# An S6 scan kernel on one Trainium2 core: the residual is added in PSUM by TensorE and copied out by ScalarE, where VectorE added it before

## What is computed

```
x = x + s6(layernorm(x))
x = x + ffn(layernorm(x))      # a routed feed-forward block on 127 rows of each batch

# s6: delta, B and C are projections of its input u
h = exp(delta * A) * h + delta * B * u     # 16 states for each of 512 channels, along 1024 steps
y = sum over states of h * C  +  u * D
```

## Time and profile before

| | |
|---|---|
| median of 3 runs | 4733.67 us (4727.59 to 4733.85) |
| the profiled execution's own time | 4730.44 us |
| its span in the profile | 4728.3 us |
| DVE busy in the span | 3868.9 us, 82% |
| POOL busy | 3543.6 us, 75% |
| PE busy | 2806.7 us, 59% |
| ACT busy | 2752.0 us, 58% |
| mean granted TensorE clock | 0.663 |

### The profile page before, as it was taken

The page is one execution under the profiler, slowest core; times in us unless marked ns, Lnnn a source line. Parts: engine busy times, 40 slices in busy tenths (PEclk is TensorE's granted clock), DMA queues, the critical chain, the costliest instruction groups (busy, mean ns, idle before and its releaser), DMA issues. The chain is left out here.

```text
span 4728.3 us, 57323 instructions
## 1 busy us (share of the span) xinstructions
PE 2806.7 (59%) x15590; PEld 1068.8 (23%) x15590; DVE 3868.9 (82%) x3306; ACT 2752.0 (58%) x4103; POOL 3543.6 (75%) x1796
## 2 busy tenths in 40 slices
PE   3555464546464645555454546464642399999997
PEld 1111111111121111111111111111110255555553
DVE  3999999999999999999999999999997644444442
ACT  5676766766767667676766766767754222222221
POOL 4999999999999999999999999999995100000000
PEclk7556565656565656556565656565655599999998
DMA  4454545364544545454545364545533200000000
GB/s 101 96 130 116 142 104 154 85 160 100 147 114 129 131 112 133 111 130 116 141 105 155 82 160 100 146 112 133 135 93 114 82 14 18 18 18 18 18 18 7
DMA packets 198209, 472.73 MB, mean 100 GB/s; under 512 B 60688, under 2 KB 61200, under 8 KB 197088
## 3 DMA queue, kind: packets, MB, share of 16 engines
q1 hardware_dynamic: 177136, 452.11, 37.8%
q0 software_dynamic: 20736, 16.88, 1.3%
HBM read 126.83 MB, written 73.43 MB: 42 GB/s over the span
## 5 line engine op out<-in xcount | busy, mean ns | idle before, releaser
L879 POOL TENSOR_TENSOR ch<-hid,cmat 128x1024 f32<-128x1024 f32 x1024 | 2387.2, 2354 | 101.0 <-DVE hid L733 84.1
L733 DVE TENSOR_TENSOR_SCAN hid<-decay,inp 128x1024 f32<-128x1024 f32 x1024 | 2289.2, 2274 | 96.3 <-ACT decay L600 94.2
L600 ACT ACTIVATE decay<-delr,a_neg 128x1024 f32<-128x1024 f32 x1024 | 1136.7, 1112 | 811.8 <-DVE hid L733 801.0
L399 PE MATMUL ps_y<-ch,nsum 128*32 128x256 f32 x8192 | 1000.3, 588 | 854.9 <-POOL ch L879 850.9
L722 DVE TENSOR_TENSOR inp<-dx,bmat 128x1024 f32<-128x1024 f32 x832 | 959.3, 1211 | 63.2 <-ACT dx L608 63.2
L399 PEld LDWEIGHTS ps_y<-ch,nsum 128*32 128x32 f32 x8192 | 249.0, 143 | 1591.5 <-POOL ch L879 1364.2
L408 PE MATMUL ps_y<-ident,ysb 128*128 128x128 f32 x512 | 168.9, 431 | 683.3 <-ACT ysb L615 666.7
L844 POOL TENSOR_TENSOR inp<-dxr,bmat 128x1024 f32<-128x1024 f32 x192 | 452.4, 2356 | 0.0
L1133 POOL DMA_INDIRECT out_rows<-row,idx_out x16 | 41.1, 2570 | 458.9 <-issue 252.4
L394 PE MATMUL ps_y<-xhT,dskip 128*32 128x256 f32 x2048 | 271.9, 623 | 142.5 <-DVE xr L743 142.5
L408 PEld LDWEIGHTS ps_y<-ident,ysb 128*128 128x128 f32 x512 | 71.3, 196 | 909.4 <-ACT ysb L615 865.9
(11 more groups left out here) (167 smaller groups left out, 3921.7 us busy)
## 6 DMA issues: line engine op xcount, KB each, us to landing
dxr<-dxT SPq DMA_DIRECT2D x1024, 128.0 KB, 2.4
delr<-delT SPq DMA_DIRECT2D x1024, 128.0 KB, 2.4
xr<-in_x SPq DMA_DIRECT2D x32, 1024.0 KB, 5.5
bmat<-b_and_c SPq DMA_DIRECT2D x256, 128.0 KB, 3.4
cmat<-b_and_c SPq DMA_DIRECT2D x256, 128.0 KB, 2.9
x_rows<-xr SPq DMA_DIRECT2D x16, 2048.0 KB, 7.6
out_rows<-xr SPq DMA_DIRECT2D x32, 1024.0 KB, 4.3
w<-in_w SPq DMA_DIRECT2D x2, 4096.0 KB, 23.7
```

Of the source, the lines that this page charges most:

```text
L399: last = pe.matmul(ps_y[q * CH:(q + 1) * CH, 0:2 * P], nsum[:], ch[:, g, q * 2 * P:(q + 1) * 2 * P], start=False, stop=(g == GROUPS - 1))
L600: nc.scalar.activation(decay[:, g % 2, :], delr[:, c % 2, :], ACT.Exp, scale=a_neg[:, i:i + 1])\
L733: nc.vector.tensor_tensor_scan(hid[:, g, :], decay[:, g % 2, :], inp[:, g, :], 0.0, ALU.mult, ALU.add).then_inc(hid_ready, 1)
L879: nc.gpsimd.tensor_tensor(ch[:, g, :], hid[:, g, :], cmat[:, g, :], ALU.mult).then_inc(ch_ready, 1)
```

## The change

VectorE's add is gone. Instead `turn_y` makes each half of the turned output by two matmuls that accumulate in PSUM: one multiplies `ysb` by the identity (this turns it), the second multiplies the identity by the slice of `xr` and adds it on top. ScalarE then copies the sum from PSUM over `xr` (`copy_x1`), which now raises `y_added`. In ScalarE's order `copy_x1` stands right behind `copy_dx`. The transposes were `pe.transpose`; the two that replace them are plain fp32 matmuls, since the second must accumulate.

```diff
-            def turn_y(b, c):
+            def turn_y(b, par, c):
                 pe.wait_ge(ysb_ready, b * CHUNKS + c + 1)
                 for t in range(2):
-                    last = pe.transpose(ps_y[:, (2 + t) * P:(3 + t) * P], ysb[:, t * P:(t + 1) * P], ident[:])
+                    out_t = ps_y[:, (2 + t) * P:(3 + t) * P]
+                    x_t = xr[:, par, :, c * CH:(c + 1) * CH].rearrange("p (q t) d -> p t q d", t=2)[:, t]
+                    pe.matmul(out_t, ysb[:, t * P:(t + 1) * P], ident[:], start=True, stop=False)
+                    last = pe.matmul(out_t.rearrange("p (q d) -> p q d", q=4), ident[:], x_t, start=False, stop=True)
                 last.then_inc(yt_ready, 1)
...
+            def copy_x1(b, par, c):
+                act.wait_ge(yt_ready, b * CHUNKS + c + 1)
+                if c == 0:
+                    act.wait_ge(xh_ready, b * TC + TC)
+                nc.scalar.activation(xr[:, par, :, c * CH:(c + 1) * CH].rearrange("p (q t) d -> p t q d", t=2),
+                                     ps_y[:, 2 * P:4 * P].rearrange("p (t q d) -> p t q d", t=2, q=4),
+                                     ACT.Copy).then_inc(y_added, 1)
...
                     if not (final and c == CHUNKS - 1):
                         copy_dx(*nxt)
+                    if c > 0:
+                        copy_x1(b, par, c - 1)
+                    elif has(b, 1):
+                        copy_x1(b - 1, 1 - par, CHUNKS - 1)
                     beside(b, par, c, 1)
...
             copy_y(last, CHUNKS - 1)
+            copy_x1(last, 1, CHUNKS - 1)
             copy_rw(last)
...
                     for g in range(GROUPS):
                         scan(b, c, g)
-                        if g == YADD:
-                            if c >= 1:
-                                add_y(b, par, c - 1)
-                            elif has(b, 1):
-                                add_y(b - 1, other, CHUNKS - 1)
...
-            add_y(last, 1, CHUNKS - 1)
```

More of the change, by code:

```diff
@@ L29 @@
 HALF = 512
-YADD = 2
 TURN = ((7, 1), (7, 2), (8, 0), (8, 1), (8, 2), (9, 0), (9, 1), (9, 2))
@@ L424, in body @@
                     if c > 0:
-                        turn_y(b, c - 1)
+                        turn_y(b, par, c - 1)
                     elif has(b, 1):
-                        turn_y(b - 1, CHUNKS - 1)
+                        turn_y(b - 1, 1 - par, CHUNKS - 1)
                     for g in range(GROUPS):
@@ L447, in _ @@
             batches(pe, body)
-            turn_y(nb_run - 1, CHUNKS - 1)
+            turn_y(nb_run - 1, 1, CHUNKS - 1)
             pe.wait_ge(wcol_ready, nb_run)
@@ L734, in scan @@
                                              0.0, ALU.mult, ALU.add).then_inc(hid_ready, 1)
[L736 to L743, removed]
             def router(b, par, h):
```

## The result

The changed kernel takes 4744.82 us (median of 11 runs, 4738.67 to 4748.27) against 4733.67 us for the kernel before (median of 11 as well): ratio 1.0023, 95% interval 1.0014 to 1.0032. It is slower by 11 us, 0.23%. The profiled execution takes 4741.05 us, and its span is 4739.0 us, 10.7 more than before. The forecast was 4721, faster, with a range of 4702 to 4744: the time lies 0.8 us above the range's upper end. The rival with ScalarE's queue as the bound had 4746.

What follows compares the result with a forecast made beforehand. GpSimd, working about 97% of a batch, was taken to bound the kernel. Small waits -20, last batch -6, loaded stretch +12 and end +1 gave -13 us from 4733.67: 4721, range 4702 to 4744.

Steps and rivals of the forecast that it cites:

- The rival with ScalarE's queue as the bound: Chunks 15 to 2: two copies each hold ScalarE 0.85 us longer, growth 2.5 us a batch, +13, 4746; chance 0.18.
- Its price of VectorE's add: Gain from freeing VectorE: 20 us from GpSimd's small waits over fifteen batches, 6 us in the last batch.
- the dry places at 12 to 15: GpSimd's waits for VectorE late in a batch; those at chunks 12 and 13 should go, 15 x 1.35 = 20 us.
- The last batch: No step sizes to make there, VectorE sets the end: it gains 1.7 us of waits and 4.4 of adds, together 6.
- Its prices of the parts: Lower clock: turn 2.0 us in place of 0.69, ScalarE standing 1.25 us, copy 0.36 us, each copy_x1 delaying ScalarE 1.6 us.
- The fourfold transposes: Rival: transposes four times cheaper than plain matmuls, turn 3.7 us, +38 us, 4771; chance 0.03.
- In chunks 3 to 12 ScalarE has waits for VectorE to swallow this: Chunks 3 to 12: ScalarE's 1.6 us delay behind each copy costs nothing, being absorbed by its waits for VectorE.
- The rival "the lead does not carry": Another wait, such as a projection at chunks 10 and 11, holds VectorE; dry places stay at half, 0, 4734; chance 0.17.
- So the cap doesn't bite: ScalarE's queue caps VectorE's lead, but about 8.5 us of work fits within GpSimd's at least 11.6 us of tiles.
- the loaded stretch: Chunks 15 to 2, ScalarE busy with step sizes and layernorm sums: GpSimd's chunk-3 wait grows 0.8 us, 15 times, +12 us.
- 0.5 are left: Chunk 15: of ScalarE's delay there, 0.5 us remains after the 0.90 us wait takes part, and carries into chunk 0.
- the case of 4704: Rival: TensorE's clock rises in the loaded stretch, shortening the turn; -30 us, 4704; chance 0.18.

Runs made afterwards that it cites:

- experiment 1: Changed kernel with the residual left out and the turn back to two transposes; ScalarE still copies, VectorE adds nothing: 4698.10 us, 0.9931 of the kernel before.
- experiments 2: Kernel before with the addition left out: nobody adds or copies, and those who waited for the add wait for the turn, TensorE for nothing: 4696.49 us, 0.9924.
- Experiment 8: ScalarE copies and TensorE adds only in chunks 3 to 9; elsewhere the kernel before's transposes and VectorE's add: 4717.18 us, 0.9966 of the kernel before.
- experiment 10: Kernel before with nobody adding or copying, but with the changed kernel's turn of eight instructions: 4708.90 us, 0.9949 of the kernel before.
- experiment 5: Changed kernel with the residual's matmuls moved right behind the chunk's skip term, ahead of the turn: 4728.28 us, 0.9993 of the kernel before.
- experiment 9: Changed kernel without the residual, with the two-transpose turn, and ScalarE's copy one place later, behind the next chunk's tile-0 decay: 4778.20 us, 1.0096 of the kernel before.
- experiment 12: ScalarE copies only in chunks 3 to 9, the old way elsewhere, plus cmat reloaded one tile earlier: 4709.64 us, 0.9951 of the kernel before.

## Why the prediction was wrong

**Its price of VectorE's add was right, a little low.** It counted 20 + 6 = 26 us; experiments 1 and 2 gain 33 and 35. With a short turn the dry places at 12 to 15 do go, as it said: 14 x 1.35 = 19 us. The last batch gives 4.2, and chunks 0 and 3, which it left out, 0.2 and 0.35 a batch.

**Its prices of the parts were right.** The turn of eight instructions: 2.0 us forecast, 1880.78 to 1882.85 = 2.07 measured. ScalarE's standing: 1.25 forecast, 232.5 / 191 = 1.22 measured. The strided copy: 0.36 taken, 0.38 to 0.39 measured. The wait at L521 is gone, and VectorE waits 6.37 us in chunk 2 (5 to 7 forecast). The fourfold transposes are out: a transpose passes in 0.215 us, and plain instructions of the same columns, at 1881.36, 1881.79 and 1882.22, start 0.43 us apart by pairs, 0.215 each, two for one. The Trainium skill ("TensorE: Matmul & The Clock Gate", Terms) has a factor of four; by these rows it is two.

**The step that failed first** is "In chunks 3 to 12 ScalarE has waits for VectorE to swallow this". By its own figure each copy makes ScalarE 1.6 us later. The waits that should swallow this are uneven, and the kernel before shows it. Means over 14 batches, worked out from the timelines, us a batch:

| chunk | 3 | 4 | 5 | 6 | 7 | 8 | 9 | 10 | 11 | 12 | 13 | 14 |
|---|---|---|---|---|---|---|---|---|---|---|---|---|
| before: ScalarE waits for VectorE | 8.6 | 5.2 | 5.5 | 1.1 | 1.3 | 1.1 | 2.0 | 4.0 | 1.9 | 3.3 | 0 | 2.4 |
| before: VectorE waits for a decay | 0 | 0 | 0 | 0 | 0 | 0 | 0 | 0 | 0 | 0 | 0.5 | 0 |
| experiment 1: VectorE waits for a decay | 0 | 0 | 0 | 0 | 0 | 0 | 0 | 0 | 0.2 | 0 | 0.9 | 0 |
| changed: VectorE waits for a decay | 0 | 0 | 0 | 1.0 | 0.8 | 0 | 0 | 0 | 0.7 | 0 | 1.9 | 0.5 |

In chunks 6 to 8 ScalarE has 1.1 to 1.3 us, less than 1.6, and in 13 it has nothing. Before, ScalarE at the start of chunk 7, in one batch:

```profile
847.40 1.12 ACT L600 ACTIVATE decay<-delr,a_neg 128x1024 f32<-128x1024 f32 x1 [0.24 <-DVE hid L733]
849.58 1.12 ACT L600 ACTIVATE decay<-delr,a_neg 128x1024 f32<-128x1024 f32 x1 [1.06 <-DVE hid L733]
```

After, VectorE in chunks 7 and 13 of that batch, a projection and a step size of ScalarE between them, and GpSimd behind them:

```profile
853.17 4.47 DVE L749 TENSOR_TENSOR_SCAN hid<-decay,inp 128x1024 f32<-128x1024 f32 x2 [0.76 <-ACT decay L602]
...
901.25 0.59 ACT L494 ACTIVATE xpT<-aux 96x512 f32<-96x512 f32 x1 [5.93 <-PE aux L372]
...
925.28 2.36 POOL L880 TENSOR_TENSOR ch<-hid,cmat 128x1024 f32<-128x1024 f32 x1 [0.52 <-DVE hid L749]
927.45 1.04 ACT L526 ACTIVATE tu<-tu 128x1024 f32<-128x1024 f32 x1
928.56 2.34 POOL L854 TENSOR_TENSOR tu<-tu,te 128x1024 f32<-128x1024 f32 x1 [0.93 <-ACT tu L526]
929.68 4.47 DVE L749 TENSOR_TENSOR_SCAN hid<-decay,inp 128x1024 f32<-128x1024 f32 x2 [2.30 <-ACT decay L602]
```

From chunk 7 to 12 VectorE is rid of six adds, 2.0 us. It pays 0.8 of them back in chunk 7 and 0.7 in chunk 11 as waits for ScalarE. GpSimd still runs dry at chunks 12 and 13, and once more, 0.93 us here, for a step size that ScalarE brings late. The forecast of 15 x 1.35 = 20 us for these places came in as 14 x 0.58 = 8. ScalarE's 5.93 us for a projection is no sign of the change: the kernel before waits up to 4.9 us there and experiment 1, which has no dry place, up to 5.7; over twelve batches the projections cost ScalarE 78.8 us before, 84.2 in experiment 1 and 86.7 in the changed kernel. The rival "the lead does not carry" had the result for these places, "at half", but the projection that it named has only a small part in it. Experiment 8 shows 0.8 us of waiting at chunk 7 too: in 3 to 9 most of the copy's delay is swallowed, not all.

A step beside it was wrong without harm. "So the cap doesn't bite" looked for a cap on VectorE's lead in ScalarE's queue. There is one in GpSimd's: the fourth input tile (L845), for which VectorE waits at chunks 5 and 6, 2.0 us a batch in the changed kernel and 3.1 in experiment 1. What VectorE gains before chunk 6 is lost there in all these versions, and the dry places depend on what it gains after.

**The step that failed second** is the loaded stretch. "0.5 are left" after chunk 15 was followed only forward to chunk 3, and priced at +12. GpSimd already waits longer in chunk 0, where the forecast put nothing: +0.93 us a batch, 13 us over 14 batches. At chunks 2 and 3 it found +0.57 a batch, 8 us, in place of 12. Together +21. The boundary where it shows most, the only one of the twelve at which GpSimd waits for TensorE (GpSimd, then ScalarE and TensorE):

```profile
1648.29 2.35 POOL L880 TENSOR_TENSOR ch<-hid,cmat 128x1024 f32<-128x1024 f32 x1 [4.46 <-PE ps_y L398]
```

```profile
1645.81 0.38 ACT L624 ACTIVATE xr<-ps_y 128x256 f32<-128x256 f32 x1 [1.98 <-PE ps_y L410]
```

```profile
1646.24 1.08 PE L393 MATMUL ps_y<-xhT,dskip 128*32 128x256 f32 x8 [0.47 <-ACT xr L624]
1647.10 1.93 PE L398 MATMUL ps_y<-ch,nsum 128*32 128x256 f32 x16
```

Here GpSimd needs a `ch` buffer that the sum must first empty; the sum waits for the copy, and the copy for the turn. With nobody copying, experiment 10 has 1.05 us at chunk 0, against 0.61 before and 1.54 here: about half of the growth there comes with the longer turn alone.

**The sum by what was measured.** -8 (chunks 12 to 15) + 13 (chunk 0) + 8 (chunks 2 and 3) = +13 for 14 batches, 14.3 by the period; start +1.5, last batch -4.3 (forecast -6), end +0.95 (forecast +1): +12.5 by the end of the scan phase against a forecast of -13. The two terms that were mis-sized are the gain at 12 and 13 (-20, it was -8) and the loaded stretch (+12, it was +21). The rival "ScalarE's queue" had 4746, right to 1 us, and its place, chunks 15 to 2, is where most of the loss is. The number is luck: it let the growth be 2.5 us a batch, and the growth is 1.5; the rest of its result is the gain that didn't come. Of the two reasons that it gave, the strided copy is as fast as the plain one but for 0.03 us, and "the skip matmuls now wait for ScalarE" isn't borne out: they wait 91.3 us, less than the 107.7 for VectorE before. Two small slips of the sum don't matter: a growth of 0.3 gives -20.5 and not -22, and 4733.67 + 38 is 4772. The forecast's own test ("wrong if GpSimd shows new waits at chunks 0 to 2, or the dry places at 12 and 13 stay") came out on both counts.

**The clock** rose a little, but not where the turn stands. A window around the turn at 1880.78 of the changed kernel, then twelve batches of the kernel before and of the changed one (PEclk is the third figure from the end):

```profile
1878.00:1887.00 9.00, 7.49 (x28) 3.12 (x28) 7.91 (x6) 7.60 (x14) 9.00 (x5) 0.50 0.97 276
500.00:3160.00 2660.00, 1410.22 (x8822) 412.96 (x8822) 2531.38 (x1775) 1853.24 (x2721) 2579.72 (x1260) 0.58 0.50 125
500.00:3160.00 2660.00, 1529.08 (x9931) 671.76 (x9929) 2448.47 (x1575) 1891.47 (x2897) 2567.45 (x1253) 0.64 0.49 124
```

Over the span the mean is 0.710 against 0.663 before. In 1878 to 1887, where the turn of chunk 1 stands, it is 0.50, and the turn took the 2.07 us of the lower level; so it did in every chunk but 8 to 11, where it took 1.2 to 1.9 (means by chunk). So the case of 4704 did not come. The cleanest pair is experiments 2 and 10, which differ in the turn alone: 0.652 with two transposes, 0.718 with eight plain instructions. The Trainium skill, "TensorE: Matmul & The Clock Gate", "Part 4: PE-mode transpose", has it that a transpose doesn't count as busy in the same way for the clock. These means agree with it in direction, no more: the plain turn also has four times the instructions, and no run here tells the kind from the amount.

**What stays open.** How the 34 us divide between ScalarE's standing and TensorE's late opening is not isolated. The traces favour the standing: against experiment 1 ScalarE's waits for the turn grew by 210 us and its waits for TensorE's other work fell by 26, and experiment 5, which cut the standing to 69.4 us, won 14 us back although it made that other work later. A release that doesn't depend on the copy, with the copy in its place, wasn't tried.

## What to carry to other kernels

Before moving a step to another engine, read that engine's slack place by place, at the place where the step will stand. ScalarE waited for VectorE 46.6 us in a batch of the kernel before, and still had too little in chunks 6 to 8 and none in 13. Then ask which semaphore moves with the step: its place in the new in-order queue has a price on both sides. Too early, and the engine stands (1.22 us a chunk here); one place later, and whoever waits for the semaphore is late (80 us in experiment 9). A chain of two engines that each wait for the other (copy, turn, copy, release) costs more than its parts: 12 us and 2 us alone, 48 together. Where an engine has slack in only some of the iterations, move the work only there: the split of experiment 8, with experiment 12's reload, turned +0.23% into -0.49%.

## What was not expected of the hardware

At some batch boundaries, where the program loops back, SyncE's eight issues of cmat take longer. Its timeline at two boundaries of the changed kernel:

```profile
1415.78 3.76 SPq L289 DMA_DIRECT2D cmat<-b_and_c  x8
...
1640.76 5.96 SPq L289 DMA_DIRECT2D cmat<-b_and_c  x8
```

Every second boundary takes 4.9 to 6.3 us (1640.76, 2086.44, 2531.87, 2978.25), the others 3.8; in the kernel before it was 4.6 to 4.9 against 3.8. In 1638 to 1650 the DMA view of the changed kernel shows packets of instruction code on two further queues:

```profile
q8 instruction: 2, 0.03, 1.3%
q14 instruction: 4, 0.03, 0.7%
```

At the boundary of 1412 to 1425, where the issues take 3.76 us, there is one packet on q8 and none on q14. That fetching code is what slows the issues is my reading of their coming together; no run here removes the fetch. It can't be all: the kernel before has 2 and 5 such packets at its boundary of 1628 to 1640 and takes 4.7 us there, not 6.
